# A cast moved to the front of ScalarE's step, GpSimd's sum of the rotation moved across a step border, and a transpose moved ahead of two projections on TensorE, in a two-block transformer kernel

## The reference

```python
x = x + xattn0(layernorm(x), ctx, ctx)        # 16 heads of 8, rotary embedding on Q and K
x = x + ffn0(layernorm(x))                    # 128 -> 512 -> 128, ternary weights, relu
x = x + xattn1(layernorm(x), ctx, ctx, mask)  # 16 query heads, 4 key/value heads, causal mask and
                                              # given mask, layernorm of the heads' output
x = x + moe(layernorm(x))                     # 8 experts, top 1 of a softmax gate, gelu
```

```python
Q, K, V = query @ Wq.T, key @ Wk.T, value @ Wv.T
Q, K = rope(Q), rope(K)
out = softmax(Q K^T / sqrt(8)) V @ Wo.T
```

## Time and profile before

| | |
|---|---|
| median of 3 runs | 702.67 us |
| the profiled execution's own time | 701.69 us |
| its span in the profile | 699.9 us |
| TensorE busy (share of the span) | 559.8 us (80%) |
| VectorE | 432.9 us (62%) |
| ScalarE | 350.9 us (50%) |
| GpSimd | 323.2 us (46%) |

### The profile page before, as it was taken

How to read it: one execution, slowest core, us unless ns; L and a number is a source line. 1 busy time by engine, 2 the same in 40 slices (tenths; PEclk the granted TensorE clock), 3 DMA queues, 4 the chain that set the end, 5 groups by cost and what they waited for, 6 DMA issues and landing times.

```text
span 699.9 us, 19715 instructions
## 1 busy us (share of the span) xinstructions
PE 559.8 (80%) x6015; PEld 371.6 (53%) x6016; DVE 432.9 (62%) x1361; ACT 350.9 (50%) x839; POOL 323.2 (46%) x529
## 2 busy tenths in 40 slices
PE   1478887988877699958999999999883881499993
PEld 0345555665554599933444444444431450399993
DVE  6458787899876566436676667767753548044441
ACT  2127565766655255624556565565441521166662
POOL 6754444454420466554354353444313177255563
PEclk9959999999999699969999999999997765599998
DMA  6243333333324700022222222222100024233331
GB/s 188 67 106 94 97 92 85 91 97 97 91 72 152 196 1 0 1 76 73 74 60 72 70 64 56 75 71 55 48 7 1 4 104 161 73 92 92 97 98 33
DMA packets 97517, 54.01 MB, mean 77 GB/s; under 512 B 23138, under 2 KB 93538, under 8 KB 97458
## 3 DMA queue, kind: packets, MB, share of 16 engines
q1 hardware_dynamic: 94674, 46.45, 25.2%
q0 software_dynamic: 2784, 6.82, 2.7%
HBM read 19.79 MB, written 8.81 MB: 41 GB/s over the span
## 4 chain that ended last, share of the span: by engine, by line
PE 50%; SPq 11%; issue 10%; POOL 10%; DVE 7%; ACT 5%; DMA 5%; POOLq 0%; ACTq 0%; DVEq 0%
PE score L535 5%; PE scoreT L535 5%; PE bank L808 5%; PE bank L610 5%; SPq L365 4%; ACT P L893 4%; PE scoreT L693 4%; DVE negmax L1298 4%; SPq L376 4%; PE score L558 4%; PE bank L703 4%; PE scoreT L796 3%; PE scoreT L576 3%; POOL expert_rows L1188 3%; POOL piece L1101 2%
## 5 line engine op out<-in xcount | busy, mean ns | idle before, releaser
L1298 DVE TENSOR_REDUCE negmax<-score 128x8 f32<-128x1024 f32 x128 | 156.3, 1221 | 47.0 <-PE score L558 46.5
L893 ACT ACTIVATE P<-scoreT 128x1024 f32<-128x1024 f32 x128 | 131.1, 1024 | 53.5 <-PE scoreT L576 34.0
L1101 POOL TENSOR_TENSOR piece<-full,piece 128x256 bf16<-128x256 f32 x64 | 42.8, 669 | 192.3 <-ACT piece L874 192.3
L610 PE MATMUL bank<-P,Vc 128*32 128x128 f32 x2048 | 82.9, 280 | 0.4
L558 PE MATMUL score<-Ks,Qs 64*128 64x128 bf16 x1024 | 52.9, 225 | 21.9 <-DMA Ks<-piece 11.5
L899 ACT COPY outs<-bank 128x256 f32<-128x256 f32 x64 | 23.6, 369 | 80.3 <-PE bank L610 80.1
L558 PEld LDWEIGHTS score<-Ks,Qs 64*128 64x128 bf16 x1024 | 32.0, 97 | 58.4 <-issue 51.2
L1203 POOL DMA_INDIRECT out<-by x39 | 39.9, 1022 | 37.1 <-POOL by L1197 21.8
L610 PEld LDWEIGHTS bank<-P,Vc 128*32 128x32 f32 x2048 | 48.4, 109 | 14.4 <-ACT P L893 0.9
L535 PE MATMUL score<-mask,negI 128*128 128x512 bf16 x128 | 40.3, 397 | 11.2 <-issue 5.9
L1324 DVE RECIPROCAL rden<-bank 128x16 f32<-128x16 f32 x64 | 16.5, 257 | 51.3 <-PE bank L625 50.9
(11 more groups left out here) (195 smaller groups left out, 1220.5 us busy)
## 6 DMA issues: line engine op xcount, KB each, us to landing
Qs<-piece SPq DMA_DIRECT2D x192, 64.0 KB, 2.0
Ks<-piece SPq DMA_DIRECT2D x96, 64.0 KB, 2.0
ctxT<-in_ctxT SPq DMA_DIRECT2D x32, 128.0 KB, 2.2
XB<-expert_rows SPq DMA_DIRECT2D x39, 66.0 KB
XA<-expert_rows SPq DMA_DIRECT2D x39, 64.0 KB
XR<-in_x SPq DMA_DIRECT2D x4, 512.0 KB, 4.6
Qs<-blank SPq DMA_DIRECT2D x32, 64.0 KB, 2.0
Qs<-negpT SPq DMA_DIRECT2D x64, 32.0 KB, 1.9
```

The lines of the kernel that those rows point to most:

```text
L610: mm = nc.tensor.matmul(PVOUT[VCOL * i:VCOL * (i + 1), half * 128:(half + 1) * 128], Vc[:, k % BODY, at:at + VCOL], P32[:, c, i * 128:(i + ...
L893: nc.scalar.activation(P32[:, half * 2:half * 2 + 2, :], SCORET[:], ACT.Exp, scale=SCALE).then_inc(sem("exp_done"), 1)
L1101: nc.gpsimd.tensor_tensor(pc[0:m, 1, :], f, h, ALU.subtract).then_inc(sem(f"{nm}_pieces"), 1)
L1298: nc.vector.tensor_reduce(negmax[:, k % 2, :, half * HQ:(half + 1) * HQ], SCORE[:].rearrange("p r (h k) -> p r h k", h=HQ), AX.X, ALU.max, ...
```

## The change

Three orders are changed, and no instruction is added or taken away. On TensorE `regroup(t - 1)` stands before the first half of the projection and no longer between the halves. On ScalarE `high` stands first in the step and no longer after the evictions of maxima and outputs. On GpSimd, in the first attention, `cut` comes first in a step and `whole` after it; `whole` takes the pair that the next step's `cut` needs. The first two hold for both attentions.

```diff
@@ TensorE, step @@
                     max_transpose(t + 1)
                     out_transpose(t - 2)
+                    regroup(t - 1, j - 1)
                     project(j, 0)
-                    regroup(t - 1, j - 1)
                     project(j, 1)
                     scoresT(t, 1, j)
@@ ScalarE, step @@
                 def step(t, j):
+                    if j % 2 == 0:
+                        high(j + 4, 1)
+                    else:
+                        high(j + 5, 0)
                     evac_outs(t - 1)
                     exps(t, 0)
                     evac_max(t + 1, j + 1)
                     evac_out(t - 2)
-                    if j % 2 == 0:
-                        high(j + 4, 1)
-                    else:
-                        high(j + 5, 0)
                     exps(t, 1)
@@ GpSimd, step @@
                     k, which = (j + 4, 1) if j % 2 == 0 else (j + 5, 0)
+                    cut(k, which)
                     if L == 0:
-                        whole(k, which)
-                    cut(k, which)
+                        if j % 2 == 0:
+                            whole(j + 6, 0)
+                        else:
+                            whole(j + 5, 1)
                     if L and j % 2 == 0:
                         add_bias(j + 6)
```

## The result

The changed kernel takes 701.6 us as the median of 20 runs (697.95 to 706.37); the kernel before, run beside it, takes 705.52 us (701.23 to 710.9). The ratio is 0.9947, 95% interval 0.9926 to 0.9967: 0.5% faster. Forecast were 0.7% and 698.1 us, against a median of 702.67 from three runs; with seventeen more it is 705.52.

A forecast was written before the change was run, and what follows sets the result against it. SyncE's copy queue was taken to bound the first attention, TensorE to be busy in the second. Against the profiled 701.69 us, -1.1 - 4.5 + 1.0 = -4.6 gave 697.1, as median 698.1; own range 695.5 to 700.5, 8-in-10 range 692.5 to 705.5.

The forecast's parts named there:

- rival B: No change: other delays replace SyncE's closed holes, the second attention costs 1 us; median 701 to 702; chance 0.25.
- signs listed for a wrong prediction: TensorE idle before line 634 for VectorE's split, second-attention pairs over 13.5 us, or SyncE's pairs near 10.8 with holes gone.
- Part 1, the sum: GpSimd's `whole` after `cut`: acts only at the first attention's beginning, K stack at 32.16 instead of 33.30; -1.1 us.
- Rival D: GpSimd's reordered `whole` gives a step more of lead in the steady part; no chance given.
- Part 2, the cast, first attention: ScalarE's `high` first: pieces about 2 us earlier, SyncE's 6.8 us of holes close, pair 10.24; -4.5 us net.
- The +2.3 us: First attention, even steps: GpSimd's K cut collides with VectorE's split, 0.2 us for each of some 11 pairs.
- Part 2, the collision in the second attention: GpSimd's earlier cut delays VectorE's split in odd steps; one or two collisions cost nothing; +1.0 us, ends 0 and +11.
- The price of three: Second attention, odd steps: three collisions, up to 1.9 us, exceed the hidden 1.28; 0.4 to 0.8 us a step, 14 times.
- Part 3, the transpose: TensorE's `regroup` ahead of the projections: 0 us, ends -0.1 and +0.1 a step where ScalarE's eviction is late.
- rival A: Slower: three split collisions per odd step hold TensorE at line 634 in the second attention; 706 to 711 us; chance 0.17.
- Rival C: All of 6.8 + 1.1 us gained, collisions free, freed split gives 1 us more; 693.8 us; chance 0.15.

The follow-up runs named there:

- the variants that keep the second attention whole: Against the kernel before: all three orders, first attention only, 0.9895; ScalarE's and GpSimd's orders only, 0.9912; changed kernel with TensorE's old order in second attention, 0.9903.
- the copy added: Changed kernel plus one 64 KB copy of zeros issued by SyncE per Q stack of the first attention; 1.0128 to the kernel before.
- the copy taken off it: ScalarE's and GpSimd's orders changed, first attention's zeros copy issued by ScalarE instead of SyncE, with its own semaphore; 0.9744 to the kernel before.
- cast and sum: Kernel before with ScalarE's `high` and GpSimd's `whole` moved in their steps, TensorE's `regroup` left between the projection halves; 0.9912 to the kernel before.
- the sum alone: Kernel before with only GpSimd's order changed, `cut` first and `whole` after it; 0.9970 to the kernel before.
- the cast alone: Kernel before with only ScalarE's order changed, `high` first in the step in both attentions; 0.9907 to the kernel before.

## Why the prediction was right, and where it was wrong

The change in time was right: 0.65% forecast, 0.53% measured. It is partly luck, since two terms were off in opposite ways: the variants that keep the second attention whole are 6.2 to 7.4 us faster than before, where the sum had 5.6 for the first attention, and the second lost 5.1 and not 1.0. In us the forecast of 698.1 was 3.5 too low, outside its own 695.5 to 700.5, and the measured 701.6 is where rival B had put it; that is the higher median of the kernel before and not rival B's mechanism, as said below. Of the signs listed for a wrong prediction one came true, pairs of the second attention over 13.5 us (13.83); the idle time before line 634, named beside it, did not.

- **What bounds the kernel.** Right. SyncE's queue bounds the first attention, shown by the copy added (+10.4 or more) and by the copy taken off it (-9.2 against cast and sum).
- **Part 1, the sum.** Right to 0.1 us: forecast -1.1 and a first K stack at 32.16 (32.1 in the list of signs), found 32.13, and both of its halves are there (Q -0.57, K -1.17); 10.75 us a pair with the sum alone confirms that the edit does nothing in the steady part. Rival D is out.
- **Part 2, the cast, first attention.** The mechanism is right: the holes of 6.8 us are gone. The term was -4.5; the first profiles give -4.64 + 1.17 = -3.5, the means of all profiles -7.3 + 1.2 = -6.1, and SyncE's queue by itself, in the first profiles, -5.2. The pair was to be 10.24, and is 10.24 and 10.39 (median of the last five of the loop). The queue's first stretch has 62 issues and not 63, which changes nothing. The odd steps' split is freed as said: lines 1307 and 1314, 407 and 573 ns before, are 174 and 168 (as 1310 and 1317, both steps). The last subtraction meets the cut in 6 of 24 steps and takes 0.67 us there. The +2.3 us that the sum had for this collision show nowhere: the gaps of the queue fell by 6.5 of the 6.8 us. Against the gain stand 1.3 us of longer issues.
- **Part 2, the collision in the second attention.** The mechanism and its number are right: two collisions in an odd step, split done 0.68 us late, line 634 without a wait, exactly the case that was held to cost nothing. And by itself it costs nothing (13.39 a pair with the cast alone). The price of three was miscounted: 1.9 us less the hidden 1.28 is 0.6 and not up to 0.8, so the ends of +11 here and in rival A were a little too wide. The rule of the Trainium skill (SBUF — State Buffer, "Who interferes with whom") is borne out: the prolonged operations have two SBUF inputs and end with GpSimd's operation, while the reduction from PSUM stays at 1.21 us beside the same cut.
- **Part 3, the transpose: the step that failed.** "0 us, ends -0.1 and +0.1 a step where the eviction is late by the cast". The sum asks what the moved instruction waits for on ScalarE, and doesn't go through its other waits. `regroup` waits for the values in odd steps; in the second attention VectorE makes them, behind the maxima that the collision delays. Each of the two edits had slack enough for itself, 0.48 us in each of 12 odd steps is what they lack together. Measured: +5.06 us where the sum had +1.0 for the collision and 0 for the transpose. Rival A named the right stage, the slower side and the first link, but the wrong place of the wait (line 634, from three collisions on) and so wrong conditions.
- **Rival B** is out, since no other delay took the place of the holes: what issues over 0.9 us last beyond their 0.6 is 8.7 us in the changed kernel's profile and 7.6 before. **Rival C** (1.3% by its 693.8) happened in the first attention nearly as priced: with the second attention kept whole, the three variants are 0.9 to 1.05% faster.
- The median of before rested on 3 runs; over 20 it is 2.9 us higher. A forecast in us carries that error, one in per cent doesn't.

## What to carry to other kernels

When two orders are changed at once, list every wait of each moved instruction, and add the delay that the other edit puts on what it waits for; here each was free alone and together they cost 5 us. Before moving an instruction to the front of an in-order queue, ask which semaphore it waits on and whether it counts work that the instruction doesn't need: one shared semaphore made the difference between 1.001 and 0.974. And where a DMA-issuing queue has no gaps left, count its issues: closing its holes gave 0.5 us a pair, moving one copy to another engine's queue 0.4 more.

## What the runs showed of the hardware

- An issue of a copy of 64 KB holds SyncE's queue for 0.60 us (median) and 0.04 between two, while the DMA engines are busy for 0.35 to 0.38 of the time: an added copy costs 0.70 to 0.85 us a pair. One issued by ScalarE took 0.54 us beside its activations, and with a semaphore of its own the pair got 0.40 us shorter.
- Nine or ten of the 243 issues last over 0.9 us; from 45 to 120 us, in the steps written out and in the first turn of the loop, they come every 6 to 18 us, from 120 to 180 us there is none, and behind the loop they are back (both profiles of the kernel before and both of the changed one).
- Operations of VectorE with 16 elements per partition and two SBUF inputs take 0.17 us alone and 0.5 to 0.67 us beside GpSimd's subtractions. At the border of two operations of GpSimd without a gap such an operation gets through (the ends at 404.90 and 405.55 follow GpSimd's at 404.87 and 405.52, and a third one took 0.16 us from 404.82): a chain of three was delayed by 0.68 us, not by three whole operations.
